# Order of VectorE's and TensorE's instructions in a retention layer between two FFNs: masks together, turn of gn between the value halves, group means before the norm

## What is computed

```python
x = x + 0.5 * ffn(layernorm(x))
x = x + attn(layernorm(x))
x = x + 0.5 * ffn(layernorm(x))

# ffn: I = 768; weights rounded to float8_e4m3 values
down(silu(h @ gate_w * gate_s) * (h @ up_w * up_s)) * down_s

# attn: 16 heads of 16 channels
q, k, v = split(h @ w_qkv); q, k = xpos(q), xpos(k)       # a rotation by position
scores = (q @ k.T) * 16 ** -0.5 * decay_mask              # causal, gamma_h ** (t - s), no softmax
y = scores @ v
yn = (y - mean_16(y)) / sqrt(var_16(y) + 1e-5) * gn_w + gn_b   # per row and head
return (silu(h @ w_g) * yn) @ w_proj
```

## Time and profile before

| | us |
|---|---|
| median of three runs | 178.29 (178.2 to 178.42) |
| the profiled execution, its own time | 178.39 |
| its span (first to last instruction) | 176.6 |
| TensorE busy, its weight loads | 163.6 (93%), 124.8 (71%) |
| VectorE busy | 137.0 (78%) |
| ScalarE busy | 75.6 (43%) |
| GpSimd busy | 67.6 (38%) |
| chain that ended last | TensorE 59%, VectorE 23%, issue 6%, ScalarE 5% |
| scores of tile 0 start, of tile 7 start | 60.98, 125.34 |

### The profile page before, as it was taken

How to read it: one execution, slowest core, us unless ns; L and a number is a source line. 1 busy time by engine, 2 the same in 40 slices (tenths; PEclk the granted TensorE clock), 3 DMA queues, 4 the chain that set the end, 5 groups by cost and what they waited for, 6 DMA issues and landing times.

```text
span 176.6 us, 3264 instructions
## 1 busy us (share of the span) xinstructions
PE 163.6 (93%) x1125; PEld 124.8 (71%) x1125; DVE 137.0 (78%) x294; ACT 75.6 (43%) x162; POOL 67.6 (38%) x76
## 2 busy tenths in 40 slices
PE   5997989899899999998999999999889899799992
PEld 2355756688779776866686868777658688798881
DVE  2899899999834395778696969979778797765763
ACT  3153498767205024233434160614616546225510
POOL 3445293453844311334462827463495420000000
PEclk9999999999999999999999999999999999999999
DMA  5898105403000000000000000000000000011002
GB/s 158 282 347 295 64 2 175 181 4 121 0 4 0 0 0 4 0 0 4 2 0 4 2 0 0 4 0 6 0 0 2 0 4 0 0 59 59 6 30 89
DMA packets 6848, 8.41 MB, mean 48 GB/s; under 512 B 416, under 2 KB 5552, under 8 KB 6832
## 3 DMA queue, kind: packets, MB, share of 16 engines
q1 hardware_dynamic: 6832, 8.20, 13.7%
HBM read 7.15 MB, written 1.05 MB: 46 GB/s over the span
## 4 chain that ended last, share of the span: by engine, by line
PE 59%; DVE 23%; issue 6%; ACT 5%; POOL 3%; DMA 2%; SPq 0%; DVEq 0%; ACTq 0%
PE bank L991 15%; PE bank L1019 9%; PE bank L1112 8%; PE bank L1047 6%; DVE fuse L660 3%; PE bank L1168 3%; DVE sc L715 3%; PE bank L1058 3%; PE bank L1061 3%; PE bank L1090 2%; PE bank L1106 2%; DVE grid L574 2%; DVE h L632 2%; DMA xt<-in_L_attn_x 2%; PE bank L1073 2%
## 5 line engine op out<-in xcount | busy, mean ns | idle before, releaser
L991 PE MATMUL bank<-hh,gate_r 128*128 128x512 f32 x96 | 27.9, 408 | 3.6 <-DVE hh L644 2.1
L991 PE MATMUL bank<-hh,up_r 128*128 128x512 f32 x96 | 26.3, 396 | 0.0
L1019 PE MATMUL bank<-down_r,fhi 128*128 128x256 f32 x96 | 24.3, 291 | 0.3 <-DVE flo L668 0.3
L324 POOL TENSOR_TENSOR grstd<-gve,neg_half 128x16 f32<-128x16 f32 x8 | 23.3, 2907 | 0.7
L1019 PE MATMUL bank<-down_r,flo 128*128 128x256 f32 x96 | 23.4, 282 | 0.0
L991 PEld LDWEIGHTS bank<-hh,gate_r 128*128 128x128 f32 x96 | 16.7, 188 | 9.5 <-issue 3.8
L408 ACT ACTIVATE gact<-bank,vec 128x512 f32<-128x512 f32 x24 | 16.5, 686 | 16.0 <-PE bank L991 15.7
L660 DVE SCALAR_TENSOR_TENSOR fuse<-bank,vec,gact 128x512 f32<-128x512 f32 x24 | 17.9, 746 | 5.3 <-PE bank L991 5.1
L991 PEld LDWEIGHTS bank<-hh,up_r 128*128 128x128 f32 x96 | 18.1, 188 | 4.2
L715 DVE TENSOR_TENSOR sc<-bank,msk 128x512 f32<-128x512 f32 x32 | 20.3, 682 | 0.0
L1019 PEld LDWEIGHTS bank<-down_r,fhi 128*128 128x128 f32 x96 | 18.1, 188 | 1.2 <-DVE flo L668 0.6
(11 more groups left out here) (80 smaller groups left out, 301.0 us busy)
## 6 DMA issues: line engine op xcount, KB each, us to landing
raw<-in_rotation SPq DMA_DIRECT2D x1, 1536.0 KB, 6.5
xt<-in_L_attn_x SPq DMA_DIRECT2D x2, 512.0 KB, 4.6
out<-xt SPq DMA_DIRECT2D x8, 128.0 KB, 1.7
raw<-in_L_ffn_down_w SPq DMA_DIRECT2D x2, 384.0 KB, 7.6
wqkv<-in_L_attn_w_qkv SPq DMA_DIRECT2D x1, 768.0 KB, 9.4
raw<-in_rotation SPq DMA_DIRECT2D x1, 512.0 KB, 3.3
raw<-in_L_ffn_gate_w SPq DMA_DIRECT2D x1, 384.0 KB, 6.1
raw<-in_L_ffn_up_w SPq DMA_DIRECT2D x1, 384.0 KB, 6.7
```

Of the source, the lines that this page charges most:

```text
L324: pool.tensor_tensor(grstd[:, c % 2], gve[:, :], neg_half[:, :], ALU.pow).then_inc(grstd_done, 1)
L991: mm = pe.matmul(dst[:, :], wr[m][:, k * I + i * P:k * I + (i + 1) * P], half[:, k, g % NG, :], start=(k == 0 and half is hhi), stop=(k == ...
L1019: mm = pe.matmul(downs[d][:, 0:C], half[:, g % NG, i, t * P:(t + 1) * P], wr["down"][:, i * C:(i + 1) * C], start=(i == 0 and half is fhi) ...
```

## The change

It changes the order of instructions on VectorE and on TensorE and nothing else; no instruction is added or taken away. On VectorE, in tiles 0 to 6, the four masks stand in a row, with `add_proj` and `group_norm` behind them; `group_mean(c-1)` comes at the end of iteration c, ahead of the `norm_tile` of that iteration, where it stood at the beginning of iteration c+1; the `norm` of tiles 0 to 2 for the second FFN comes at the end of iteration 5 where it was in iteration 6. Behind the loop the masks of tile 7 stand in a row after `group_mean(6)` and `group_var(5)`; the statistics of rows 4 and 5 for the second FFN go behind `group_norm(7)`, and `rest_h(3)` goes ahead of a `rest_f` and a `fuse_up`. On TensorE, `turn_gn(c-2)` stands between `values(c, 0)` and `values(c, 1)`, and `turn_qk(c+1)` ahead of `turn_y(c-1)`.

```diff
--- before.py
+++ after.py
@@ -856,22 +856,17 @@
             scale_down(7)
             for c in range(NT - 1):
                 if c >= 2:
-                    group_mean(c - 2)
                     group_var(c - 2)
                 rotate_parts(c + 1)
                 mask_kv(c)
-                mask_scores(c, 0)
-                mask_scores(c, 1)
+                for r in range(HG):
+                    mask_scores(c, r)
                 if c >= 3:
                     add_proj(c - 3)
+                if c >= 2:
+                    group_norm(c - 2)
                 if c == NT - 2:
                     norm_stats(2 * NT + TH - 1, 2 * NT + TH)
-                if c >= 2:
-                    group_norm(c - 2)
-                mask_scores(c, 2)
-                mask_scores(c, 3)
-                if c == NT - 2:
-                    norm(2 * NT, 2 * NT + TH - 1)
                 rotate(c + 1)
                 if c + 3 < NT:
                     norm_stats(NT + c + 3, NT + c + 4)
@@ -881,19 +876,20 @@
                     norm_tile(2 * NT + TH - 1)
                 if c >= 2:
                     gated(c - 2)
+                if c >= 1:
+                    group_mean(c - 1)
                 if c + 3 < NT:
-                    norm(NT + c + 3, NT + c + 4)
+                    norm_tile(NT + c + 3)
+                elif c == NT - 3:
+                    norm(2 * NT, 2 * NT + TH - 1)
 
             c, j0 = NT - 1, NG * NI
-            group_mean(c - 2)
+            group_mean(c - 1)
             group_var(c - 2)
-            group_mean(c - 1)
-            mask_scores(c, 0)
-            mask_scores(c, 1)
+            for r in range(HG):
+                mask_scores(c, r)
             group_var(c - 1)
             add_proj(c - 3)
-            mask_scores(c, 2)
-            mask_scores(c, 3)
             rest_h(2, 0)
             group_norm(c - 2)
             rest_h(2, 1)
@@ -906,10 +902,9 @@
             add_proj(c - 2)
             rest_f(j0)
             fuse_up(j0 + 1)
-            norm_stats(2 * NT + TH, 2 * NT + TH + 1)
             group_norm(c)
             add_proj(c - 1)
-            norm_stats(2 * NT + TH + 1, 2 * NT + TH + 2)
+            norm_stats(2 * NT + TH, 2 * NT + TH + 2)
             gated(c)
             rest_f(j0 + 1)
             fuse_up(j0 + 2)
@@ -921,10 +916,10 @@
             norm(3 * NT - 2, 3 * NT)
             rest_f(j0 + 3)
             fuse_up(j0 + 4)
+            rest_h(3, 0)
+            rest_h(3, 1)
             rest_f(j0 + 4)
             fuse_up(j0 + 5)
-            rest_h(3, 0)
-            rest_h(3, 1)
             rest_f(j0 + 5)
             for i in range(NI):
                 fuse_up(j0 + NI + i)
@@ -1214,13 +1209,13 @@
                 project_vg(c + 1)
                 if c + 2 < NT:
                     turn_h2(c + 2)
+                values(c, 0)
                 if c >= 2:
                     turn_gn(c - 2)
-                values(c, 0)
                 values(c, 1)
+                turn_qk(c + 1)
                 if c >= 1:
                     turn_y(c - 1)
-                turn_qk(c + 1)
                 if c + 2 < NT:
                     project_qk(c + 2)
                 if c + 1 < NT - 1:
```

## The result

The changed kernel takes 173.34 us (median of four runs, 172.83 to 173.99) against 178.35 (178.2 to 178.6); the ratio is 0.9722 with a 95% interval of 0.9691 to 0.9754. The prediction was 173.4 within 172.5 to 175.1. The profiled execution has a span of 171.8, 4.8 less than before. The page of the changed kernel (first lines, and the costliest group of GpSimd) shows the same instructions in a shorter span.

A forecast was written before the change was run, and what follows sets the result against it. VectorE's order was taken to bound the tile at 9.62 us, with TensorE's own 9.12 next. Gains of 1.50+0.97+0.73+0.65+0.09+0.92 = 4.86 took the median from 178.29 to 173.43, range 172.5 to 175.1.

The forecast's parts named there:

- The loop: Tiles 3 to 5: VectorE's order bounds the tile at 9.62; the altered loop is 8.66, so TensorE's 9.12 bounds next.
- Tiles 3 to 5: Each tile takes 9.12 us for 9.62: a gain of 0.50 each, 1.50 together.
- Tile 2: Tile 2 takes 8.66 us for 9.63, a gain of 0.97.
- Tile 6: Scores of tile 6 to those of tile 7: 8.61 for 9.34 us, gain 0.73 (1.05 if no lock).
- The lock: Two-SBUF-input VectorE and SBUF-reading GpSimd instructions exclude each other: go held by add_state in tile 6, later steps +0.36.
- Tile 7: From tile 7's scores to the second FFN's first gate load: 6.31 for 6.96 us, gain 0.65.
- The two waits for gn: Up to the gate load at 139.25: TensorE waits 0.6 (0.17 before), then 0.71 (1.25 before); net gain 0.09.
- rest_h(3): Second FFN: the 1.46 gate wait for hh goes, flo(17) is next late; down products 151.52 for 152.44, gain 0.92.
- The first: Rival: TensorE's full column is right, the values' first half takes 1.09 by its own pace; 174.9 us; 10%.
- The second: Rival: the loop's gain comes, but tiles 6 and 7 and hh give back what follows; 175.8 us; 10%.
- The third: Rival: slower, 178.65 us and up, through the loop of gsum, turn_y, affine copies and gn, put at 8.29; 5%.
- The sum: Whole kernel: 1.50+0.97+0.73+0.65+0.09+0.92 = 4.86 us gained, for a median of 173.43.

The follow-up runs named there:

- the mean behind h: The changed kernel with the group mean behind the norm of h at the end of each tile: 175.19 us, ratio to before 0.9813.
- The experiment on gvar: The changed kernel with group_var(5) ahead of group_mean(6) behind the loop: 172.74 us, ratio to before 0.9684.

## Why the prediction was right

**The loop.** It was read as 9.62 before, 8.66 after, with TensorE's own 9.12 as the next bound. That its terms add up to the 9.62 between the scores proves nothing, though the prediction offers it as proof: a walk from turn_qk to the turn_qk a tile later gives the period of any kernel. What was at stake were the altered loops. Measured 9.62 and 9.08; turn_gn between the halves loads in 0.17 and not in the 0.22 that I carried over, which is the difference. Two kernels that undo one side each, and two that do one side alone, came out at the loop's figure within 0.05 (9.57 for 9.56, 9.69 for 9.74, 9.90 for 9.91, 9.95 for 9.96), so it is shown that the loop through VectorE's order was the bound. That TensorE's own pace is the bound now rests on the loads without waits and on the mean behind h, where masks 0.3 later cost nothing. Tiles 3 to 5 gave 1.62 for the 1.50 forecast. Tile 2 gave 1.08 for 0.97: about half of the difference is turn_gn again, the rest that its masks end at S+3.78 for S+3.85.

**Tile 6.** 0.49 instead of 0.73. The lock was counted, at the right size (0.41 measured, 0.36 forecast) but on the wrong instruction: I had it hold go, with two inputs in SBUF, and took h, a tensor_scalar with one, to be free of it. It was h that started 0.06 behind add_state and took 0.82, and go came free. turn_y(6) loads at S6+8.48 for the 8.40 that the forecast means (8.04 and 0.36). The rest of the miss is from there to the scores: 0.21 forecast, like the 0.22 from turn_y(7) to a gate load in the earlier trace rows, and 0.37 measured (122.14 to 122.51); what fills it is not shown. There is a slip in the forecast, too: 8.29 and 0.36 are 8.65 and not 8.61, so its gain should have read 0.69. The same lock was forecast to hold rotate in the tiles before, hidden but for 0.34 in tile 5. There rotate starts first and keeps its length, and add_state is the one stretched, to 1.03, which costs nothing.

**Tile 7.** 0.84 instead of 0.65: the masks start at S7+1.23 where the forecast has 1.39, so the later scores were partly caught up. Both together 1.33 against 1.38.

**The two waits for gn behind it.** 0.6 and 0.71 were forecast, 0.75 and 0.72 came, and the stage stayed as it was (6.96 for 6.95; forecast 0.09 less). The experiment on gvar shows that the first is GpSimd's series of grstd.

**rest_h(3).** 0.95 for 0.92, with flo next as forecast (a wait of 0.42, where the forecast's 1.3 and 0.92 mean 0.38). Its sum has a slip as well: 149.3, 0.75, 0.63 and 0.68 make 151.36 and not 151.46.

**Rivals.** The first, TensorE's column taken at its word, would have kept 9.6 in tiles 3 to 5; it is out. The second, later stages giving back, is out: they brought 2.27 of the 4.97. The third needed turn_y's path to be over 9.12 long; it was put at 8.29, and with turn_y ahead tiles got longer, not shorter.

**The sum** was 4.86 and the stages gave 4.97. That it is so close is in part luck: the terms were off by +0.12 (tiles 3 to 5), +0.11 (tile 2), -0.24 (tile 6), +0.19 (tile 7), -0.10 (the two waits) and +0.03 (rest_h), which cancel. The medians differ by 5.01 and the profiled executions by 4.79, which is the 4.97 less 0.36 for the late first scores, with 0.2 back at the end.

## What to carry to other kernels

When two engines write out their orders by hand, follow one item around (here turn_qk, gvar, masks, values, turn_qk). The distances always add up to the period; the loop is the bound, however full a column is, only if no step has slack: here gvar started as soon as the squares were there, gn as soon as grstd was, the masks and what stood between them back to back, and the load 0.61 behind the last mask. Then an instruction costs what it stands in the way of, and the loop with one order altered can be added up and tried. In the changed kernel the same loop has 0.53 of slack (the masks end at 99.28, 0.61 later is 99.89, and TensorE needs them at 100.42). Reordering one engine alone can then be worse than nothing, since the other still queues the freed work behind what has just become late: masks in a row and turn_gn between the halves cost 0.7% and 0.8% apart and gave 2.8% together with the rest. Compare kernels by distances between their own marks: stages that a move doesn't touch repeated to 0.02 us, where four executions of the changed kernel lie between 172.83 and 173.99.

## What the runs showed of the hardware

VectorE's tensor_scalar with one SBUF tensor and two scalars per partition as inputs (h, 128x256 float32) is held by GpSimd's sum of two SBUF tensors as a tensor_tensor is: 0.82 us beside it and 0.41 without. The Trainium skill's page "SBUF — State Buffer" (Who interferes with whom) lists tensor_scalar among the instructions that can enter a 2-port mode and then contend; the trace agrees, and I had left that half of the rule out. In the other direction add_state took 1.03 instead of 0.73 when rotate was under way. The three h of the earlier trace rows had been beside an add_state as well, but started when only 0.32 of it was left (120.85 to 121.58), and took 1.12 for the 1.05 of three h in the changed kernel (from 112.40, with no add_state beside them).

That the later one waits for the whole instruction, as the prediction has it, does not hold for GpSimd's power (grstd, 128x16), though its two inputs are in SBUF. In the kernel before gn, with two SBUF inputs, ran inside one, and both kept their lengths:

```profile
129.77 2.90 POOL L324 TENSOR_TENSOR grstd<-gve,neg_half 128x16 f32<-128x16 f32 x1
...
130.38 0.41 DVE L753 TENSOR_TENSOR gn<-gd,grstd 128x256 f32<-128x256 f32 x1
```

In the changed kernel go, with two SBUF inputs, ran at its usual length inside it, and grstd took 3.00 instead of 2.90:

```profile
127.56 3.00 POOL L324 TENSOR_TENSOR grstd<-gve,neg_half 128x16 f32<-128x16 f32 x1
...
129.72 0.42 DVE L761 TENSOR_TENSOR go<-ga,sg 128x256 f32<-128x256 f32 x1
```

gn was still under way when this grstd started (127.39 to 127.80), so which of the two cost it the 0.10 is open. In what part of its time such a power can hold VectorE, if in any, was not tried.
